# Nine 16-bit products of zeros on TensorE in every pass but the first, in layers 0 and 1 of a graph attention kernel

## The reference, cut to what matters

```
h  = (x @ W).reshape(N, 8, 32)
el = einsum('nhd,hd->nh', h, al);  er = einsum('nhd,hd->nh', h, ar)
e  = leaky_relu(el[src] + er[dst], 0.2)
ex = exp(e - segment_max(e, dst)[dst])
a  = ex / segment_sum(ex, dst)[dst]
out = segment_sum(h[src] * a[:, :, None], dst) + b
```

## Time and profile before

| | |
|---|---|
| median of the runs | 9250.0 us |
| the profiled execution's own time | 9270.94 us |
| its span | 9269.2 us |
| TensorE busy, mean granted clock | 65% of the span, 0.80 |
| VectorE, ScalarE, GpSimd busy | 51%, 18%, 49% |
| DMA | 909.79 MB, 98 GB/s mean |

### The profile page before, as it was taken

One profiled execution on the slowest core, in us unless ns is written; L12 is line 12 of the kernel. 1 busy time (PEld: TensorE's weight loads), 2 busy tenths in 40 slices (PEclk: granted clock), 3 DMA queues, 4 the chain that ended last, 5 costly groups with the idle time before them and its releaser, 6 DMA issues.

```text
span 9269.2 us, 139557 instructions
## 1 busy us (share of the span) xinstructions
PE 6004.1 (65%) x27934; PEld 4636.2 (50%) x27935; DVE 4741.8 (51%) x10724; ACT 1700.8 (18%) x4763; POOL 4543.3 (49%) x4723
## 2 busy tenths in 40 slices
PE   4555555555665555555565665566777778888888
PEld 2334434444444344444444453345556666767777
DVE  5445555555555445555555564454544444444444
ACT  2000000000110000000000000012333444445454
POOL 1655555555554665555555554555444433333332
PEclk8677778778787677777777776678888999999999
DMA  5444444434443444444443444443333322222221
GB/s 177 114 111 111 111 108 113 106 103 104 108 107 95 116 111 113 109 108 111 107 111 99 104 108 95 110 110 93 90 87 79 80 74 72 69 68 66 64 61 43
DMA packets 638573, 909.79 MB, mean 98 GB/s; under 512 B 271425, under 2 KB 484554, under 8 KB 638410
## 3 DMA queue, kind: packets, MB, share of 16 engines
q0 software_dynamic: 226368, 676.39, 28.6%
q1 hardware_dynamic: 369546, 192.99, 8.8%
q10 hardware_dynamic: 42624, 40.02, 1.3%
HBM read 868.05 MB, written 40.87 MB: 98 GB/s over the span
## 4 chain that ended last, share of the span: by engine, by line
issue 21%; PE 20%; DMA 13%; SPq 12%; DVE 10%; DVEq 10%; another core or an unknown queue 9%; ACT 3%; ACTq 2%; POOL 1%; POOLq 0%
DMA dstb<-dst_d 13%; PE bank L1285 10%; SPq L332 5%; PE bank L1211 5%; PE bank L1222 3%; DVEq L241 3%; DVE msg L992 2%; SPq L334 2%; DVEq L980 2%; DVE sel L1000 2%; DVE selT L968 1%; SPq L326 1%; SPq L340 1%; ACT region L444 1%
## 5 line engine op out<-in xcount | busy, mean ns | idle before, releaser
L358 POOL DMA_INDIRECT gat<-table,meta x4716 | 4542.2, 963 | 4636.2 <-SPq L340 3066.4
L1285 PE MATMUL bank<-msg,sel 128*128 x10560 | 3761.3, 515 | 2365.0 <-DVE sel L1000 1708.3
L1285 PEld LDWEIGHTS bank<-msg,sel 128*128 128x128 f32 x10560 | 2522.7, 251 | 3020.6 <-issue 2516.7
L992 DVE SCALAR_TENSOR_TENSOR msg<-bank,gat 128x1056 f32 x1320 | 1658.2, 1256 | 856.7 <-ACT bank L487 636.9
L1000 DVE TENSOR_TENSOR sel<-iota_t,meta 128x512 f32<-128x512 f32 x1320 | 906.2, 686 | 775.2 <-remote 459.4
L487 ACT ACTIVATE bank<-lg 128x32 f32<-128x32 f32 x1320 | 261.3, 198 | 5476.9 <-DVE lg L986 3750.5
L979 DVE TENSOR_REDUCE lg<-bank 128x64 f32<-128x192 f32 x1320 | 466.5, 353 | 849.6 <-remote 607.7
L1257 PEld LDWEIGHTS bank<-uvb,selT 128*128 128x128 bf16 x5292 | 329.7, 106 | 1121.0 <-issue 563.3
L1257 PE MATMUL bank<-uvb,selT 128*128 (+1 forms) x5292 | 390.4, 195 | 748.2 <-DVE selT L968 490.0
L984 DVE TENSOR_TENSOR lg<-gat,lg 128x64 f32<-128x64 f32 x1320 | 299.3, 227 | 967.4 <-issue 520.6
L1211 PE MATMUL bank<-xT,w 128*128 128x128 f32 x6272 | 782.6, 279 | 16.1 <-issue 16.0
(11 more groups left out here) (188 smaller groups left out, 2133.1 us busy)
## 6 DMA issues: line engine op xcount, KB each, us to landing
dstb<-dst_d SPq DMA_DIRECT2D x1179, 128.0 KB
gat<-table,meta POOLq DMA_INDIRECT x4716
meta<-in_edges SPq DMA_DIRECT2D x1179, 4.0 KB
table<-hrow ACTq DMA_DIRECT2D x98, 140.0 KB
w<-in_W SPq DMA_DIRECT2D x2, 4096.0 KB
table<-hrow SPq DMA_DIRECT2D x49, 140.0 KB, 1.8
region<-xnT_d ACTq DMA_DIRECT2D x50, 128.0 KB
region<-qT_d ACTq DMA_DIRECT2D x50, 128.0 KB
```

What stands on the lines that cost most here:

```text
L358: pool.indirect_dma_start(gat[:, r, c, :], None, table[l], bass.IndirectOffsetOnAxis(meta[:, r, c, 0:1].bitcast(U32), 0)).then_inc(s_done, 16)
L992: dve_v.scalar_tensor_tensor(msg[:, bass.ds(n % 2, 1), :, :].rearrange("p a c (h d) -> p (a c) h d", h=H), ex_p.unsqueeze(3).to_broadcast( ...
L1285: last = pe.matmul(acc[:, 0:MSG], sel[:, c, :], msg[:, bass.ds(m % 2, 1), c, :].rearrange("p a m -> p (a m)"), start=opens and c == 0, sto ...
```

## The change

Layers 0 and 1 get nine more products in every pass but the first of a tile. They stand on TensorE behind `prepare_next` and ahead of the wait for the pass's `sel`. Each multiplies the zeros of `zb` (128 x 128, 16 bits) by 264 columns of `zb` and adds the result, zero, to `acc`; `start=False, stop=False` leaves the sums open. Nothing waits for them and they signal nothing.

```
+BUSY = 9
...
+                def keep_busy():
+
+                    if l + 1 < LAYERS:
+                        for _ in range(BUSY):
+                            pe.matmul(acc[:, 0:MSG], zb[:, 0:P], zb[:, 0:MSG], start=False, stop=False)
+
...
                         with pe.Fori(begin, end) as m:
                             prepare_next(m, T)
+                            keep_busy()
                             aggregate(m)
                         after(1 + part)
                     prepare_next(m3, T + 1)
+                    keep_busy()
                     aggregate(m3, closes=True)
                     after(4)
```

## The result

The changed kernel takes 9446.75 us (median of four runs, 9438.26 to 9457.34) against 9252.35 us before: a ratio of 1.0189, with a 95% interval of 1.0159 to 1.0219. I had forecast 9215 us and a range up to 9285. It is slower by 194 us, and its profiled execution has a span of 9439.0 us against 9269.2.

The account below looks back on a forecast made before the run. No engine was near full, so waits set the time. VectorE's `sel` waits, 140 us less and 56 us more, gain some 84 us, of which 0.4 reaches the end: 9250 - 35 = 9215 us, range 9130 to 9285.

Parts of the forecast that it names:

- What is added: Layers 0 and 1: 391 passes each get nine products, 7038 in all; all else stays.
- small things: Side effects: reads of `acc` move under 1 us; no row shows TensorE short of instructions, though its supply was called unknown.
- the sum: VectorE before `sel`: half of 280 us of waits go, 56 us are paid back, some 84 us gained.
- The price of a product: On TensorE, 264 columns take 0.11 us at full clock, 0.22 at low; nine take 0.99 or 1.98 us.
- What hides them: TensorE's idle time between `prepare_next` and the aggregate: 1.17 us at full clock, 1.96 or 1.00 us at low clock.
- case (c): Dense passes at the low clock: only 1.00 us is free, so the aggregate is put off by 0.98 us.
- The clock: TensorE in layers 0 and 1: half the low stretches go, clock about 0.85 instead of 0.76 and 0.73.
- The share that reaches the end: Part of VectorE's 84 us gain that shortens the kernel: 0.4, between 0.18 and two thirds, so -35 us.
- The signs I named: Expected in the profile: clock 0.82 to 0.88, `sel`'s aggregate waits from 280 to about 200 us, layer 2 unchanged.
- the ring: Loop of waits in layers 0 and 1: SyncE, GpSimd, VectorE with TensorE, and back to SyncE.
- The third rival: Slower: zeros don't raise the clock or too late, dense low-clock passes pay 0.98 us; +75 us, 9325 us; chance 0.16.
- The first rival: Gain swallowed: VectorE only waits longer for the next slot; -15 to +10 us, about 9248 us; chance 0.21.

Follow-up runs that it names:

- e3_16_columns: The changed kernel with its nine products a pass at 16 columns instead of 264: 9455 us against 9263 for the kernel before, ratio 1.0218.
- r2_after: The changed kernel measured again, in a batch where no signal is held: 7664 us against 7743 for the kernel before, ratio 0.9894.
- r_wide_logits: The kernel before with no product added, four old products of `prepare_next` widened from 48 to 480, 432, 384 and 336 columns: 9255 us against 9265, ratio 0.9980.

## Why the prediction was wrong, point by point

*The step that failed* is the first line of "What is added" together with the small things: I counted 7038 products and priced their time on the array, but I gave the 14,076 instructions themselves no price ("no row shows it short of them"). They cost about 13 ns of the end each in this place, by longer and more frequent holds of the aggregate's signal. The expected gain of 35 us has an error of 229 us. The loss of 194 us of it lies there: e3_16_columns, with products of next to no time of their own, loses as much (192 us). The other 35 us are the gain itself, which does not reach the end (see the share, below).

*The row that told it* was in my first group: `sel` stood 459.4 us for a "remote" release, more than twice the 213 us it stood for the aggregate by name. I took the 6.20 us of the earlier trace rows for a stall of VectorE. VectorE's timeline there says otherwise:

```profile
706.38 1.26 DVE L992 SCALAR_TENSOR_TENSOR msg<-bank,gat 128x1056 f32 x1
712.08 0.69 DVE L1000 TENSOR_TENSOR sel<-iota_t,meta 128x512 f32<-128x512 f32 x1 [4.44 <-remote]
```

TensorE was idle from 706.7 on, so the aggregate was over by then, `msg` ended at 707.64, and `sel` began at 712.08: it was a held signal. I worked out the sum from the named waits and left out the larger one beside them. Asking why a signal comes 5 us and more after the work that gives it would have led to what else ran then, such as GpSimd's row of gathers.

*The price of a product* was right. Nine took 1.17 us at the full clock, with the last one's end, against 0.99 reckoned from start to start; at the low clock 2.01 against 1.98.

*What hides them*: they fit as reckoned, and case (c) did no visible harm. The waits of `sel` for the aggregate in layers 0 and 1, named and unnamed together, went from 280 to some 270 us, where I expected about 200.

*The clock*: I forecast 0.82 to 0.88, it was 0.82 in both layers, at the low edge. The sum had half of the low stretches go; 0.82 leaves 36% of the time at the low level instead of 48 and 54%, so a quarter and a third went. The doubt whether products of zeros raise it is settled: they do. The Trainium skill ("TensorE: Matmul & The Clock Gate", Part 1) lets the gate go by how busy the engine is and names no condition on the values. The runs agree: 0.84 in both layers with five wide products of zeros, from 0.76 and 0.73, and 0.94 instead of 0.87 over the whole kernel in the batch of r2_after.

*The share that reaches the end* (0.4): where signals are held it is near none, 11 of 93 us of named waits in r_wide_logits, and that within noise. Where nothing is held the gain is 79 us, more than double my 35.

*The signs I named*: VectorE's idle time before L979 and L984 was to grow and fell, and SyncE's wait for `sel`, to fall from 242 us in 140 slots, rose to 584 us in 302. So the held signals did reach the ring. Layer 2 stayed within 11 us, as forecast.

*The third rival* had the sign and the wrong mechanism. It needed zeros that do not raise the clock or raise it too late, and aggregates put off by 0.98 us. The clock rose, and e3_16_columns, whose products put nothing off by that much, lost as much. *The first rival's* ground was true, the gain is swallowed, but the loss came on top.

*Two readings of GpSimd* were off, without a part in the forecast. I read 0.38 us between gathers from the rows and reckoned with 0.3, which is what the timelines show inside a row of gathers; and the 847 us for SyncE hold one wait of 168.4 us that begins before layer 0.

*What stays open*: whether GpSimd's gathers share a path with TensorE's signals and SyncE's instructions, and which, why each instruction of TensorE lengthens a hold, and what puts a batch into one condition or the other. A rival that no run tests is the profiler itself. In the long condition its trace lacks more than half of its records of semaphore changes, 58,619 in the kernel before against 135,466 in r2_after, so its own records may take part in the jam; and every execution on record was taken with its clock recorded, none without.

## What to carry to other kernels

An instruction that does nothing is not free because its time is hidden: count instructions as well as columns, and look first at waits whose releaser the profile does not find, since a signal that comes microseconds after its work shows that something other than the work sets the pace. If an engine is to be kept busy, widen instructions that are there; in this kernel that gave the clock without the loss. And a ratio measured under one condition can have the other sign under another, so the trace of the runs at hand has to show which one they are in.

## What the runs showed of the hardware

- In one condition many of TensorE's signals come late after the modelled end of its products, 520 of 1407 recorded ones by over 1 us in layers 0 and 1 of the kernel before, the latest by 14.5 us. VectorE's and ScalarE's are not late. SyncE's instructions, 0.34 us for the issue of a DMA otherwise, take up to 0.69 to 1.4 us. Both nearly end when GpSimd issues half as many gathers, in rows of at most two (7687 instead of 9257 us), and not when the gathers move half the bytes (9507 us).
- In that condition nine or eighteen loads and products added ahead of the aggregate cost about 13 ns of the kernel's end for each instruction, whether a product has 16, 132 or 264 columns; three or five cost 6 to 7 ns, and behind the aggregate it is 25 ns.
- Most of the added wait is for the next signal behind the added instructions: the aggregate's with the products ahead of it (1397 us before `sel`), that of `prepare_next` with them behind it (1510 us before L980).
- The same kernel took 7.74 ms in some batches and 9.26 ms in others, on the same two chips.
- Products of zeros raise TensorE's clock: 0.76 and 0.73 to 0.82 with nine, and to 0.84 with five wide ones. Four old products with wider operands do it too (0.82 and 0.81).
